# A chunked RWKV layer on one core: key scores and value products moved to the other half of the TensorE array

## The reference

```python
r = xrg @ Wr.T;  k = xk @ Wk.T;  v = xv @ Wv.T          # and decay w, removal a_, b_
def step(s, inp):                                       # one token, every head
    q_, w_, k_, v_, a_, b_ = inp
    sa = einsum('bhij,bhj->bhi', s, a_)
    s = s * w_[:, :, None, :] + sa[..., None] * b_[:, :, None, :] + v_[..., None] * k_[:, :, None, :]
    return (s, einsum('bhij,bhj->bhi', s, q_))
...
y = groupnorm(y) + (r * k * faaaa).sum(-1) * v          # the bonus, by head
x = x + (y * g) @ Wo.T
x = x + int8_quantised_linear(layernorm(x))
```

## Time and profile before

| what | us |
|---|---|
| median of 3 runs | 3238.7 (3226.87 to 3242.51) |
| the profiled execution, whole | 3244.0 |
| its span, first to last instruction | 3242.2 |
| PE busy | 3029.1 (93%) |
| DVE busy | 2626.5 (81%) |
| ACT busy | 1974.8 (61%) |
| POOL busy | 1270.6 (39%) |
| mean granted TensorE clock | 0.992 of full speed |

### The profile page before, as it was taken

One profiled execution on the slowest core, in us unless ns is written; L12 is line 12 of the kernel. 1 busy time (PEld: TensorE's weight loads), 2 busy tenths in 40 slices (PEclk: granted clock), 3 DMA queues, 4 the chain that ended last, 5 costly groups with the idle time before them and its releaser, 6 DMA issues.

```text
span 3242.2 us, 182735 instructions
## 1 busy us (share of the span) xinstructions
PE 3029.1 (93%) x84224; PEld 2675.6 (83%) x84224; DVE 2626.5 (81%) x5443; ACT 1974.8 (61%) x3519; POOL 1270.6 (39%) x1161
## 2 busy tenths in 40 slices
PE   6999999999999999999999999999999999999996
PEld 5888888888888888888888888888888888888884
DVE  4788888888888888887888888887888878888875
ACT  3575675665665665755656656656567566566563
POOL 4334334334334344343344343443433434433332
PEclk9999999999999999999999999999999999999998
DMA  3000000000000000000000000000000000000000
GB/s 118 10 23 20 17 23 19 18 20 18 22 20 17 23 20 17 23 20 17 22 20 19 20 17 23 20 17 23 20 17 23 20 17 20 20 20 20 16 17 19
DMA packets 39380, 70.47 MB, mean 22 GB/s; under 512 B 9812, under 2 KB 10836, under 8 KB 38616
## 3 DMA queue, kind: packets, MB, share of 16 engines
q1 hardware_dynamic: 38616, 58.77, 6.8%
HBM read 41.97 MB, written 16.78 MB: 18 GB/s over the span
## 4 chain that ended last, share of the span: by engine, by line
PE 92%; issue 3%; ACT 2%; DVE 2%; POOL 0%; POOLq 0%; ACTq 0%; DVEq 0%
PE bank L1070 30%; PE bank_a L1209 12%; PE bank L1273 8%; PE bank_a L1187 4%; PE bank L1077 4%; PE bank_b L1187 4%; PE bank_b L1244 3%; PE bank_b L1237 3%; PE bank_a L1237 3%; PE bank_a L1244 3%; PE bank_a L1217 2%; PE bank_a L1225 2%; PE bank L1123 2%; PE bank_a L1263 2%; PE bank_b L1263 2%
## 5 line engine op out<-in xcount | busy, mean ns | idle before, releaser
L504 ACT ACT_TABLE_LOAD x383 | 491.4, 1283 | 19.1 <-DVE shift L761 12.2
L1070 PE MATMUL bank<-xm_rg,w_r 128*128 128x128 f32 x2048 | 285.4, 282 | 4.3 <-issue 3.5
L504 ACT ACTIVATE u<-bank_a,parity 128x256 f32<-128x256 f32 x128 | 53.7, 471 | 386.7 <-PE bank_a L1253 386.7
L1209 PE MATMUL bank_a<-pw,w_ffn_int 32*32 32x64 f32 x16384 | 264.6, 216 | 22.0 <-issue 17.2
L1273 PE MATMUL bank<-w_o,yc 128*128 128x512 f32 x512 | 268.9, 626 | 11.0 <-DVE yc L744 9.3
L1209 PEld LDWEIGHTS bank_a<-pw,w_ffn_int 32*32 32x32 f32 x16384 | 239.6, 106 | 41.7 <-issue 21.3
L1070 PEld LDWEIGHTS bank<-xm_rg,w_r 128*128 128x128 f32 x2048 | 248.9, 191 | 26.8 <-issue 15.9
L504 ACT ACTIVATE u<-bank_b,parity 128x256 f32<-128x256 f32 x128 | 53.8, 471 | 342.3 <-PE bank_b L1253 342.3
L1070 PEld LDWEIGHTS bank<-xm_k,w_k 128*128 128x128 f32 x2048 | 241.2, 194 | 12.5 <-issue 3.8
L1070 PE MATMUL bank<-xm_v,w_v 128*128 128x128 f32 x2048 | 250.2, 275 | 0.0
L1070 PE MATMUL bank<-xm_k,w_k 128*128 128x128 f32 x2048 | 241.7, 277 | 3.5 <-issue 3.5
(11 more groups left out here) (204 smaller groups left out, 8540.4 us busy)
## 6 DMA issues: line engine op xcount, KB each, us to landing
xin<-in_x SPq DMA_DIRECT2D x128, 128.0 KB, 2.7
xres<-in_x SPq DMA_DIRECT2D x128, 128.0 KB
out<-o_sb SPq DMA_DIRECT2D x128, 128.0 KB, 2.4
w_ffn_int<-in_weight_q SPq DMA_DIRECT2D x1, 2048.0 KB, 10.8
w_k<-in_Wk SPq DMA_DIRECT2D x1, 1024.0 KB
w_r<-in_Wr SPq DMA_DIRECT2D x1, 1024.0 KB
w_v<-in_Wv SPq DMA_DIRECT2D x1, 1024.0 KB
w_o<-in_Wo SPq DMA_DIRECT2D x1, 1024.0 KB, 14.2
```

The source lines that it names most:

```text
L504: return nc.scalar.activation(out_, in_, func, **kw)
L1070: ins = mm(bank[:, o * n:(o + 1) * n], weights[:, k, o * P:(o + 1) * P], x[:, k].rearrange("p b t -> p (b t)"), start=(k == 0), stop=(k == ...
L1209: ins = mm(bank_a[q, 64 * n:64 * n + 64], pt[q, g, :], source[q, g, 0:2].rearrange("p j t -> p (j t)"), start=True, stop=True)
```

## The change

**Values in the other half.** The columns of `Wv` are loaded with the two halves of every block of 128 channels exchanged (8 DMAs in place of one), so that a head's values come out of the projection on the opposite 64 partitions.

**Scores.** Removal scores stay on the two diagonal tiles and go to `bank_a`. Key scores take the same rows but the other columns, and so land on the opposite partitions of `bank_b`. Both are issued as one stage, four matmuls for each group, one on each of the four 64x64 tiles. The stage waits for `a_b2` and `a_k2`, and both signals stand on its last matmuls.

**First state with second values.** The value products read rows of the opposite half. Those of the first chunk are a stage by themselves (`first_values`, two tiles). Those of the second chunk are interleaved with the state products of the first chunk (four tiles); the state products of the second chunk follow later (`second_state`, two tiles).

**Two copies by DMA.** `turn_keys` copies `kt` to the opposite partitions before DVE transposes it; `turn_values` copies the transposed values back to their own partitions for POOL's bonus. Each is two DMAs of 128 KB on the SP queue, from SBUF to SBUF.

**Order.** The lists of `tile_step` on PE, ACT, DVE and POOL are written in another order.

```diff
-            (w_r[:], rows("Wr")), (w_v[:], rows("Wv")), (w_gate1[:], rows("gate_w1")),
-        ]
+            (w_r[:], rows("Wr")), (w_gate1[:], rows("gate_w1")),
+        ] + [(halves(w_v[:, k])[:, :, 1 - h], halves(rows("Wv")[:, k])[:, :, h]) for k in range(KB) for h in range(2)]
...
+        def other(q):
+            return slice(P // 2 - q.start, P - q.start)
...
+
+            def turn_values(m):
+                sp.wait_ge(v_vraw, count(m, 1, 1))
+                sp.wait_ge(g_rkv, count(m, 1, 0))
+                for h in range(2):
+                    sp.dma_start(vT_own[other(two_heads(h))], vT_raw[two_heads(h)]).then_inc(v_turned, 16)
+
+            def turn_keys(i):
+                sp.wait_ge(v_k, count(i, 1, 1))
+                sp.wait_ge(v_klT, count(i, 1, 0))
+                for h in range(2):
+                    sp.dma_start(kt_turned[other(two_heads(h))], kt[two_heads(h)]).then_inc(k_turned, 16)
...
+                mul(qkT[:], vT_own[:], rk[:].unsqueeze(2).to_broadcast([P, G, HS])).then_inc(g_rkv, 1)
 
             def decayed_state(m):
...
-                dve.wait_ge(v_k, count(m, 1, 1))
-                V.transpose(km[:, :, 2, :], kt[:]).then_inc(v_klT, 1)
+                dve.wait_ge(k_turned, count(m, 32, 32))
+                V.transpose(km[:, :, 2, :], kt_turned[:]).then_inc(v_klT, 1)
                 V.transpose(first[:, :, 3, :], bt[:]).then_inc(v_blT, 1)
...
-            def scores(bank, keys_):
-                for n, g, q in head_pairs([(g, g) for g in range(G)]):
-                    ins = mm(bank[q, 64 * n:64 * n + 64], both(keys_[q, g]),
-                             both(aq[q, g, 0:2]), start=True, stop=True)
-                return ins
-
-            def scores_b(m):
+            def scores(m):
                 pe.wait_ge(v_q, count(m, 1, 1))
                 pe.wait_ge(a_b2, count(m, 1, 1))
+                pe.wait_ge(a_k2, count(m, 1, 1))
                 pe.wait_ge(a_y, count(m, NC, 0))
-                scores(bank_a, bt2).then_inc(p_sb, 1)
-
-            def scores_k(m):
-                pe.wait_ge(a_k2, count(m, 1, 1))
-                scores(bank_b, kt2).then_inc(p_sk, 1)
+                for g in range(G):
+                    for h in range(QH // 2):
+                        q = two_heads(h)
+                        removal = mm(bank_a[q, 64 * g:64 * g + 64], both(bt2[q, g]), both(aq[q, g, 0:2]),
+                                     start=True, stop=True)
+                    for h in range(QH // 2):
+                        q = two_heads(h)
+                        key = mm(bank_b[other(q), 64 * g:64 * g + 64], both(kt2[q, g]), both(aq[q, g, 0:2]),
+                                 start=True, stop=True)
+                removal.then_inc(p_sb, 1)
+                key.then_inc(p_sk, 1)
 
             def power(m, k):
                 if k == 0:
...
-            def from_values(m, c):
+            def values_product(c, j, q):
+                bank, t = step_bank(c), other(q)
+                g = j * NC + c
+                return mm(bank[q, 4 * CHUNK * j:4 * CHUNK * j + 3 * CHUNK], both(vT2[t, g]),
+                          km[t, g].rearrange("p j t -> p (j t)"), start=(j % 4 == 0), stop=False,
+                          skip_group_check=True)
+
+            def state_product(c, j, q):
                 bank = step_bank(c)
-                if c == 0:
-                    pe.wait_ge(a_vT2, count(m, 1, 1))
-                    pe.wait_ge(v_klT, count(m, 1, 1))
-                    pe.wait_ge(v_km, count(m, 1, 1))
-                if c == 1:
-                    pe.wait_ge(v_t, count(m, 1, 1))
-                for j, g, q in step_pairs(c):
-                    mm(bank[q, 4 * CHUNK * j:4 * CHUNK * j + 3 * CHUNK], both(vT2[q, g]),
-                       km[q, g].rearrange("p j t -> p (j t)"), start=(j % 4 == 0), stop=False, skip_group_check=True)
-
-            def from_state(m, c):
-                bank = step_bank(c)
-                pe.wait_ge(sold, count(m, NC, c + 1))
-                for j, g, q in step_pairs(c):
-                    ins = mm(bank[q, 4 * CHUNK * j:4 * CHUNK * j + 3 * CHUNK], both(s_old2[q, j]),
-                             aq[q, g].rearrange("p j t -> p (j t)"), start=False, stop=False, skip_group_check=True)
+                g = j * NC + c
+                return mm(bank[q, 4 * CHUNK * j:4 * CHUNK * j + 3 * CHUNK], both(s_old2[q, j]),
+                          aq[q, g].rearrange("p j t -> p (j t)"), start=False, stop=False, skip_group_check=True)
+
+            def first_values(m):
+                pe.wait_ge(a_vT2, count(m, 1, 1))
+                pe.wait_ge(v_klT, count(m, 1, 1))
+                pe.wait_ge(v_km, count(m, 1, 1))
+                for j in range(GS):
+                    for h in range(QH // 2):
+                        values_product(0, j, two_heads(h))
+
+            def first_state_second_values(m):
+                pe.wait_ge(sold, count(m, NC, 1))
+                pe.wait_ge(v_t, count(m, 1, 1))
+                for j in range(GS):
+                    for h in range(QH // 2):
+                        ins = state_product(0, j, two_heads(h))
+                    for h in range(QH // 2):
+                        values_product(1, j, two_heads(h))
+                ins.then_inc(p_rhs, 1)
+
+            def second_state(m):
+                pe.wait_ge(sold, count(m, NC, 2))
+                for j in range(GS):
+                    for h in range(QH // 2):
+                        ins = state_product(1, j, two_heads(h))
                 ins.then_inc(p_rhs, 1)
...
```

More of the change, by code:

```diff
@@ L464, in tile_step @@
                     norm_rstd(j)
+                if solve:
+                    decayed_state(m)
                 if project:
                     kept_keys(i)
-                if solve:
-                    decayed_state(m)
-                    bonus(m)
                 if finish:
@@ L472, in tile_step @@
                 if solve:
+                    bonus(m)
                     weighted_bonus(m)
@@ L674, in tile_step @@
                 if project:
+                    keys(i)
                     ma_gate(i)
@@ L712, in tile_step @@
                     solution(m, 0)
+                if mix:
+                    low_rank(j)
+                if solve:
                     output_gate(m)
@@ L982, in tile_step @@
                     token_major_values(m)
+                if mix:
+                    norm_input(j)
+                if solve:
+                    power(m, 0)
+                    scores_k(m)
+                if finish:
+                    head_norm(n)
+                if solve:
                     enter(m)
-                    power(m, 0)
+                    power(m, 1)
                 if project:
@@ L1008, in tile_step @@
                     half_inverse(m)
+                    bonus_rows(m)
+                if project:
+                    decay_sums(i)
+                if solve:
                     inverse(m)
@@ L1297, in tile_step @@
                 if solve:
-                    scores_b(m)
-                    scores_k(m)
+                    scores(m)
                 if project:
                     gates(i)
+                    queries(i, [0])
                 if solve:
@@ L1304, in tile_step @@
                 if project:
-                    queries(i, [0])
                     values(i, [0])
                     decay_gate(i)
+                    values(i, [1])
                 if solve:
```

104 lines of the change are left out of this document (51 added, 53 removed).

## The result

The changed kernel takes 3321.8 us (median of 4 runs, 3318.5 to 3326.7), the kernel before 3240.0 us on the same chip (3226.9 to 3242.5): a ratio of 1.027, 95% interval 1.025 to 1.030. Slower, where 3123 us were forecast. The profiled execution took 3326.7 us.

A forecast was written before the change was run, and what follows sets the result against it. PE was taken as the bound: 3.3 saved, 2.15 of waits and 0.8 hidden gave 1.95 us a step, 125 us in 64 steps; 3244.0 - 125 + 4 = 3123 us, range 3030 to 3230.

The forecast's parts named there:

- What bounds the kernel: Whole step: PE, busy 93% and holding 92% of the chain, bounds it, so PE time removed shortens the end.
- Four tiles at once: Scores and mixed state and value products: a round of four takes 62 ns, saving 3.3 us a step.
- Rivals 2 and 3: Four-tile rounds: about 93 ns from sharing, 3242 us, chance 0.10; or 124 ns by taking turns, 3334 us, chance 0.14.
- rival 3: Four-tile stages: tiles of the same rows take turns, a round takes 124 ns, 3334 us; chance 0.14.
- Together 2.15 us: PE's new order: its four added waits sum to 2.15 us a step, bounds 0.7 and 3.0.
- `gma`: Queries behind the gates: PE waits 0.7 us a step for ACT to end it.
- Low rank and first values: PE's low-rank and first value products: earlier PE and later ACT add 0.7 us of waits for `mix` and `vT`.
- Behind the first solution: PE waits 0.3 us a step for ACT's `lo`, with two pieces of 1.09 us as cover.
- `xm_wa`: Behind the second right-hand sides: it takes 3.85 us against PE's cover of about 3.4, a 0.45 us wait before `hidden`.
- over 3 us: Sign of being wrong: PE's waits sum to over 3 us a step.
- What the waits hide: Issue pieces ahead of the new waits: 0.8 of 1.5 us a step hidden, bounds 0 and 1.5.
- Copies and start: DMA copies of keys and values cost nothing; loading `Wv` in small pieces adds 4 us, bounds 0 and 8.

The follow-up runs named there:

- the two-tile run: Changed kernel with scores and mixed state and value products issued kind by kind, so only two tiles work at a time: 3438.5 us, ratio 1.064.
- the changed kernel with its blocks placed: Changed kernel plus 158 unused TensorE instructions a step, so instruction blocks begin at fixed places of every step: 3309.3 us, ratio 1.023.
- the edit of the front: Changed kernel with ACT's low_rank ahead of the queries and first solution, plus VectorE and ScalarE work reordered to shorten waits: 3277.7 us, ratio 1.009.
- the kernels with badly placed blocks: Changed kernel with ACT's low_rank earlier and inverse products repeated, shifting block borders: 3482.2 us (ratio 1.081) and 3683.5 us (ratio 1.135).
- the fastest kernel: Changed kernel with low_rank earlier, front and tail of the step reordered, and 158 unused TensorE instructions a step placing the blocks: 3181.7 us, ratio 0.984.
- the kernel before has 3 with its blocks placed: Kernel before, otherwise unedited, plus 160 unused TensorE instructions a step that fix where blocks begin: 3205.6 us, ratio 0.991.
- the same kernel without the blocks placed: Changed kernel with low_rank earlier and front and tail of the step reordered, without the added instructions: 3289.3 us, ratio 1.013.
- the kernel with the most stalls: Changed kernel with ACT's low_rank earlier and 158 inverse products a step issued a second time: 3683.5 us, ratio 1.135.

## Why the prediction was wrong

- *What bounds the kernel.* It took PE as the bound, which the two-tile run bears out (117 us longer). But 1.2 us a step of stalls lay between PE's records, and PE had so little slack that any new wait showed. It saw "issue" and had no cause for it.
- *Four tiles at once: right.* 58 ns from round to round and 3.16 us a step, against 62 and 3.3. Rivals 2 and 3 are refuted by the timeline, though the time that rival 3 gave (3334) is nearer than any other; a right time would have been no proof of it.
- *The waits: the step that failed.* The forecast's "Together 2.15 us" measured 3.70. `gma`: 0.7 forecast, 0.81 in PE's waits and 0.88 in the table. Low rank and first values: 0.7 forecast, 1.25 measured. Of this the wait for `vT` was put at 0.1, and its piece grew by 0.73. The sum for the low rank also counted the 0.80 us "issue" piece of the step it was read from the earlier trace rows as if every step had it; such a stall came at that source line 8 times in the whole trace. Behind the first solution: 0.3 forecast, 1.12 measured, the largest miss, because the chain was followed to `lo` and not to `hid_g`, which ACT issues two copies later and which frees a bank that the same stage writes. `xm_wa`: 0.45 forecast for the hidden product; 0.45 was measured, but at the quantised rows, whose bank is free when DVE has read `xm_wa` from it. PE waits 1.06 us there; before, it waited for `u` at about the same point, which is why the piece grew by less. In both of these places the wait was for a bank, not for data. The text had named "over 3 us" as what would prove it wrong.
- *What the waits hide: nothing in the net.* +0.8 us a step was credited. In the trace of after the stalls are as large as before (81 and 78 us), the irregular part grew by 0.30 us a step, and the granted clock's dips, up to 36 us by the estimate above, are part of it. That a stall hides ahead of a wait is true (the changed kernel with its blocks placed shows it), but the faster stages bring about as many new ones: 54 us with two tiles, 81 with four.
- *Copies and start: right.* The copies are free; the start is 4.5 us later against 4.
- *In the sum:* gain 3.16 x 64 = 202; waits 3.70 x 64 = -237; small differences 0.3 x 64 = -19; irregular part, the clock in it, 0.30 x 64 = -19; start -4.5; that is -78 of the -83 us seen, and the steps behind the last scores have the rest. Against the forecast the waits missed by 99 us, the credit for what they hide by 51, the gain by 9, and the other two terms, which it did not have, are 38: 197 of the 199 us between the forecast and the median.

The time of rival 3 came out near for another reason, and the instruction blocks, which no rival had, are the larger lesson. Had the waits been 2.15 us, as forecast, the stalls might still have taken a part: the edit of the front shortened its two pieces by 1.1 us a step (medians) and brought only 17 us.

The clock's dips have two sources here. In the changed kernel they belong to the waits: without its stalls it has 89 us of half-speed stretches, with them 85. In the kernels with badly placed blocks they grew with the stalls, to 283 and 423 us. Open is how the 51 us of the fastest kernel divide (the kernel before has 3 with its blocks placed, 14 without), what exactly the clock costs, and why a block comes sooner after the last in one place than in another. Of the 36 us of stalls that are left in the fastest kernel 26 lie at its half inverse, in 19 steps; its largest wait, 82 us for `qT`, is longer than in the same kernel without the blocks placed (58 us). Neither was followed up.

## What to carry to other kernels

When PE's waits are on "issue" and fall on runs of small matmuls, count instructions. Two packets never started less than 3.2 us apart here, and a stalled block mostly began 3.4 to 5.0 us after the last. Where 256 instructions last less than that, the stage can run at the pace of the instruction queue, and making it faster may give nothing by itself. A step whose instructions are a multiple of 256, with the borders outside the dense stages, was worth 0.4 to 2.9% here, even with useless products as the filler. And a wait moved in a list must be followed to every semaphore of the waiting instruction, banks included, not only to the data that it reads.

## What the runs showed of the hardware

- Four 64x64 tiles with float32 operands run at once: rounds of four start 58 ns apart, and so did rounds of two; 32 of them take 2.03 us, where 32 rounds of two took 2.01. The Trainium skill's rule that a weight load overlaps a matmul only where the row group differs ("TensorE: Matmul & The Clock Gate", Part 3) does not show here: two of the four tiles share their rows.
- Changing between 32x32 tiles and the full array cost 0.28 us for a visit of two records.
- PE's instructions come as 16 KB packets of 256 instructions on a queue of their own (664 packets in 3242 us). Two packets never started less than 3.2 us apart, and a stalled PE went on about 1.4 us after the end of the packet.
- The granted clock fell to a mean of 0.926 in the kernel with the most stalls (3683 us), where the kernel before has 0.992.
